# Routed rows kept as two planes of 16-bit halves and turned by a transposing DMA instead of TensorE

## What is computed

```
scores = softmax(xt @ gate_w.T)                    # 8 experts
top_vals, idx = top_k(scores, 2)
xs = xt[:, None, :] * weights[:, :, None]          # each token goes out twice, scaled
for e in range(8):
    h  = silu(xs @ w1[e].T + b1[e])
    x2 = h @ w2[e].T + b2[e]
    x3 = xs @ w3[e].T + b3[e]
    y += sum(x2 * x3 * (idx == e))
z = silu(xt @ sw1.T) * (xt @ sw2.T) @ sw3.T        # the shared expert
x = x + gb * (y + z)
```

## Time and profile before

| | us |
|---|---|
| median of 3 runs (2061.04 to 2063.82) | 2062.91 |
| the profiled execution, its own time | 2061.47 |
| its span, first to last instruction | 2059.7 |
| scatter stage, about | 1700 to 1842 |
| expert stage, first matmul of a tile to last accumulating DMA | 1844 to 2056 |

### The profile page before, as it was taken

How to read it: one execution, slowest core, us unless ns; L and a number is a source line. 1 busy time by engine, 2 the same in 40 slices (tenths; PEclk the granted TensorE clock), 3 DMA queues, 4 the chain that set the end, 5 groups by cost and what they waited for, 6 DMA issues and landing times.

```text
span 2059.7 us, 25386 instructions
## 1 busy us (share of the span) xinstructions
PE 1815.1 (88%) x6768; PEld 829.6 (40%) x6768; DVE 1923.7 (93%) x1820; ACT 1598.3 (78%) x3362; POOL 1796.3 (87%) x612
## 2 busy tenths in 40 slices
PE   7888898989797979888888989898976899999997
PEld 3323332424242423232323333332422356569996
DVE  7999999999999999999999999999999988857775
ACT  5886779898989898877788898989896744546664
POOL 5689999999999999999999999999999943545555
PEclk9998898989898989898998989898987899999999
DMA  7745454444545353536263535454445334635555
GB/s 268 229 139 145 110 137 111 129 115 112 133 110 127 106 129 106 140 88 164 68 160 89 143 92 136 111 135 115 116 105 149 100 129 137 253 134 88 97 94 75
DMA packets 140653, 263.93 MB, mean 128 GB/s; under 512 B 21840, under 2 KB 44368, under 8 KB 139488
## 3 DMA queue, kind: packets, MB, share of 16 engines
q1 hardware_dynamic: 125920, 240.58, 43.7%
q0 software_dynamic: 13296, 17.80, 5.1%
q10 hardware_dynamic: 1296, 3.93, 0.5%
HBM read 193.10 MB, written 70.19 MB: 128 GB/s over the span
## 4 chain that ended last, share of the span: by engine, by line
PE 26%; ACT 22%; DVE 19%; issue 17%; POOL 12%; DMA 4%; SPq 1%; DVEq 0%; ACTq 0%; POOLq 0%; PEldq 0%
DVE hst L1935 13%; ACT psum L1399 8%; POOL hst L1058 8%; DVE dbu L1914 5%; PE psum L2739 4%; PE psum L2495 4%; ACT dbu L1431 3%; PE psum L2925 3%; PE psum L2934 2%; PE psum L2753 2%; PE psum L2945 2%; POOL dbu L1046 2%; DMA out_x<-h,target_u 2%; PE psum L2415 1%; ACT sp_tmp L1368 1%
## 5 line engine op out<-in xcount | busy, mean ns | idle before, releaser
L1058 POOL TENSOR_TENSOR hst<-hst,c_rep 128x2048 f32<-128x2048 f32 x254 | 1145.4, 4535 | 3.9 <-ACT state L1385 3.6
L1399 ACT ACTIVATE psum<-dt_rep,neg_a 128x512 f32<-128x512 f32 (+1 forms) x1024 | 659.9, 676 | 122.7 <-DVE hst L1935 118.2
L1935 DVE TENSOR_TENSOR_SCAN hst<-psum,state,dbu 128x1024 f32<-128x1024 f32 x264 | 604.3, 2328 | 0.5 <-DVE score L2012 0.4
L1935 DVE TENSOR_TENSOR_SCAN hst<-psum,dbu 128x1024 f32<-128x1024 f32 x248 | 554.5, 2270 | 10.7 <-ACT psum L1399 10.6
L1914 DVE TENSOR_TENSOR dbu<-psum,b_rep 128x2048 f32<-128x2048 f32 x177 | 400.5, 2263 | 5.2 <-PE psum L2480 5.2
L1046 POOL TENSOR_TENSOR dbu<-dtu_rep,b_rep 128x2048 f32<-128x2048 f32 x79 | 359.4, 4549 | 8.6 <-DMA dtu_rep<-dtu_scratch 5.3
L2495 PE MATMUL psum<-hst,same 128*32 128x512 f32 x2048 | 268.8, 672 | 42.9 <-POOL hst L1058 42.9
L2480 PE MATMUL psum<-dt,same 32*128 32x512 f32 x354 | 216.5, 693 | 101.8 <-DVE dbu L1914 92.4
L2427 PE MATMUL psum<-xp,taps 128*128 128x512 f32 x512 | 237.6, 607 | 7.2 <-ACT sp_tmp L1365 6.6
L1189 POOL DMA_INDIRECT out_x<-h,target_u x71 | 111.5, 1570 | 107.1 <-issue 60.2
L1431 ACT ACTIVATE dbu<-first_decay,dbu,state 128x1 f32<-128x1 f32 x504 | 160.0, 376 | 20.8 <-DVE dbu L1914 19.4
(11 more groups left out here) (246 smaller groups left out, 2619.8 us busy)
## 6 DMA issues: line engine op xcount, KB each, us to landing
dt_rep<-dt_scratch SPq DMA_DIRECT2D x256, 256.0 KB, 4.8
dtu_rep<-dtu_scratch SPq DMA_DIRECT2D x316, 64.0 KB, 1.9
taps<-taps_scratch SPq DMA_DIRECT2D x64, 256.0 KB, 5.1
b_rep<-bc_scratch SPq DMA_DIRECT2D x64, 256.0 KB, 4.8
c_rep<-bc_scratch SPq DMA_DIRECT2D x64, 256.0 KB, 7.7
dt_scratch<-dt SPq DMA_DIRECT2D x48, 256.0 KB, 6.1
h<-slot_scratch SPq DMA_DIRECT2D x71, 129.5 KB, 2.6
sp_tmp<-t_scratch SPq DMA_DIRECT2D x16, 512.0 KB, 6.8
```

The lines of the kernel that those rows point to most:

```text
L1058: nc.gpsimd.tensor_tensor(h, h, c_rep[q % 2][:], ALU.mult).then_inc(prod_done, 1)
L1399: nc.scalar.activation(psum[:, PS_A + i, kept], dt_rep[:, G % 2, j, kept], ACT.Exp, scale=neg_a[:, q % 2, u, i:i + 1]).then_inc(exp_done, 1)
L1935: nc.vector.tensor_tensor_scan(both(hst[:, U % RING, groups, :]), both(psum[:, PS_A + 2 * pair:PS_A + 2 * pair + 2, :]), both(dbu[:, U % D ...
```

## The change

The rows in DRAM get 272 words instead of 259: the first 256 words hold the 256 float32 values as two planes of 16-bit halves, all first halves and then all second halves, and behind them stand the token number and flags. ScalarE first scales into a new buffer `weighed`, and then one more activation per `scale_tokens` splits 512 rows into the two planes of `send`. SyncE loads a tile with two DMAs: a transposing one of 128 rows by 512 halves into `turned_halves`, and a small one of 128 rows by 3 words into `xt_meta`. ScalarE's `join_halves` puts the two halves of each value side by side, SBUF to SBUF, in `xtT`, which has four buffers now. `turn_tile` and `copy_tile` are gone.

```
-ROW = DM + 1 + BATCH
+META = 1 + BATCH
+ROW = DM + 16
...
-                sp.dma_start(xt[:, s % 4, :], slot_dram[bass.ds(rows[s], P)]).then_inc(xt_loaded[s % 4], 16)
+                nc.sync.dma_start_transpose(turned_halves[:, s % 4].rearrange("p b (k c) -> p (b k) c", k=KD),
+                                            slot_halves[bass.ds(rows[s], P), 0:2 * DM]).then_inc(xt_loaded[s % 4], 16)
+                sp.dma_start(xt_meta[:, s % 4, :], slot_dram[bass.ds(rows[s], P), DM:DM + META]
+                             ).then_inc(xt_loaded[s % 4], 16)
...
             for s in range(TILES - 4):
                 sp.wait_ge(target_kept, s + 1)
                 sp.wait_ge(gate_done, s + 1)
+                sp.wait_ge(xtT_copied, s + 1)
...
+                if m >= 1:
+                    act.wait_ge(scaled, (NT + 3) * m)
...
-                    nc.scalar.activation(send[:, m % 4, tt, 0:DM], normed(p, tt), ACT.Copy, scale=weight[:, k, t:t + 1]
+                    nc.scalar.activation(weighed[:, tt, :], normed(p, tt), ACT.Copy, scale=weight[:, k, t:t + 1]
...
+                act.wait_ge(scaled, (NT + 3) * m + NT + 2)
+                nc.scalar.activation(send_halves[:, m % 4], weighed_halves, ACT.Copy).then_inc(scaled, 1)
...
-            def copy_tile(s):
-                act.wait_ge(xt_turned, s + 1)
-                if s >= 2:
-                    act.wait_ge(hx_full, s - 1)
-                nc.scalar.activation(xtT[:, s % 2, :], psum[:, s % 2, 0:DM], ACT.Copy).then_inc(xtT_copied, 1)
+            def join_halves(s):
+                act.wait_ge(xt_loaded[s % 4], 32 * (s // 4 + 1))
+                if s >= 4:
+                    act.wait_ge(hx_full, s - 3)
+                nc.scalar.activation(xtT_halves[:, s % 4], turned_halves[:, s % 4].rearrange("p b d -> p d b"), ACT.Copy
+                                     ).then_inc(xtT_copied, 1)
...
                 silu_tile(s)
-                if s + 1 < TILES:
-                    copy_tile(s + 1)
+                if s + 2 < TILES:
+                    join_halves(s + 2)
...
-            def turn_tile(s):
-                pe.wait_ge(xt_loaded[s % 4], 16 * (s // 4 + 1))
-                if s >= 2:
-                    pe.wait_ge(xtT_copied, s - 1)
-                for k in range(KD):
-                    ins = nc.tensor.transpose(psum[:, s % 2, k * P:(k + 1) * P], xt[:, s % 4, k * P:(k + 1) * P], ident[:])
-                ins.then_inc(xt_turned, 1)
...
             for s in range(TILES):
                 hidden_gate(s)
                 hidden_linear(s)
-                if s + 1 < TILES:
-                    turn_tile(s + 1)
                 if s > 0:
                     result(s - 1)
```

More of the change, by code:

```diff
@@ L10 @@
 U32 = mybir.dt.uint32
+U16 = mybir.dt.uint16
 I32 = mybir.dt.int32
@@ L215, in mixer_and_experts @@
         slot_dram = dram("slot_scratch", (SPARE + NE * P, ROW))
+        slot_halves = slot_dram.bitcast(U16)
+        slot_words = slot_dram.bitcast(U32)
         trash_dram = dram("trash_scratch", (NE * P, ROW))
@@ L391, in mixer_and_experts @@
         yt = part(8, 4, 1)
-        xtT = part(12, 2, 1)
+        xtT = part(12, 4, 1)
+        xtT_halves = xtT.bitcast(U16).rearrange("p n (d b) -> p n d b", b=2)
         hsT = part(16, 2, 1)
-        xt = flat[:, 18 * DM:18 * DM + 4 * ROW].rearrange("p (n d) -> p n d", n=4)
+        turned_halves = part(18, 4, 1).bitcast(U16).rearrange("p n (b d) -> p n b d", b=2)
+        xt_meta = flat[:, 22 * DM:22 * DM + 4 * META].rearrange("p (n d) -> p n d", n=4)
         row_gate = part(24, 2, 1)
@@ L398, in mixer_and_experts @@
         w1 = sb3("w1", [P, 2, KD, DM])
+        weighed = sb3("weighed", [P, NT, DM])
+        weighed_halves = weighed[:].bitcast(U16).rearrange("p t (d b) -> p t d b", b=2)
+        send_words = send[:].bitcast(U32)
+        send_halves = send[:].bitcast(U16)[:, :, :, 0:2 * DM].rearrange("p m t (b d) -> p m t d b", b=2)
         ffn.close()
@@ L1152, in scatter @@
                 pool.wait_ge(a_slots, m + 1)
-                pool.wait_ge(scaled, (NT + 2) * (m + 1))
+                pool.wait_ge(scaled, (NT + 3) * (m + 1))
                 for tt in range(NT):
                     nc.gpsimd.indirect_dma_start(
-                        slot_dram, bass.IndirectOffsetOnAxis(ap=slot_u[:, k, n * NT + tt:n * NT + tt + 1], axis=0),
-                        send[:, m % 4, tt, :], None).then_inc(y_stored[tt] if m == 0 else scattered[m % 4], 16)
+                        slot_words, bass.IndirectOffsetOnAxis(ap=slot_u[:, k, n * NT + tt:n * NT + tt + 1], axis=0),
+                        send_words[:, m % 4, tt, :], None).then_inc(y_stored[tt] if m == 0 else scattered[m % 4], 16)
             constants()
@@ L1736, in scale_tokens @@
                     t = n * NT + tt
-                    nc.scalar.activation(send[:, m % 4, tt, 0:DM], normed(p, tt), ACT.Copy, scale=weight[:, k, t:t + 1]
+                    nc.scalar.activation(weighed[:, tt, :], normed(p, tt), ACT.Copy, scale=weight[:, k, t:t + 1]
                                          ).then_inc(scaled, 1)
                 nc.scalar.activation(send[:, m % 4, :, DM], token_no[:, rows_of(n)], ACT.Copy).then_inc(scaled, 1)
-                nc.scalar.activation(send[:, m % 4, :, DM + 1:ROW],
+                nc.scalar.activation(send[:, m % 4, :, DM + 1:DM + META],
                                      batch_flag[:, n // SEG:n // SEG + 1, :].broadcast_to((P, NT, BATCH)), ACT.Copy
                                      ).then_inc(scaled, 1)
+                act.wait_ge(scaled, (NT + 3) * m + NT + 2)
+                nc.scalar.activation(send_halves[:, m % 4], weighed_halves, ACT.Copy).then_inc(scaled, 1)
             turned(2)
@@ L1830, in begin_gate @@
             def begin_gate(s):
-                act.wait_ge(xt_loaded[s % 4], 16 * (s // 4 + 1))
+                act.wait_ge(xt_loaded[s % 4], 32 * (s // 4 + 1))
                 if s >= 2:
                     act.wait_ge(gated, s - 1)
-                nc.scalar.activation(row_gate[:, s % 2, :], fmod[:, 0, 3, :], ACT.Copy, scale=xt[:, s % 4, DM + 1:DM + 2]
+                nc.scalar.activation(row_gate[:, s % 2, :], fmod[:, 0, 3, :], ACT.Copy, scale=xt_meta[:, s % 4, 1:2]
                                      ).then_inc(gate_begun, 1)
@@ L1842, in _ @@
                 rows_landed(act, m)
-            copy_tile(0)
+            join_halves(0)
+            join_halves(1)
             begin_gate(0)
@@ L2325, in bias_hidden @@
                                         b3[:, bass.ds(expert_of[s], 1), :], ALU.add).then_inc(hx_done, 1)
-                nc.vector.tensor_copy(target_u[:, s % IDS:s % IDS + 1], xt[:, s % 4, DM:DM + 1]).then_inc(target_kept, 1)
+                nc.vector.tensor_copy(target_u[:, s % IDS:s % IDS + 1], xt_meta[:, s % 4, 0:1]).then_inc(target_kept, 1)
             def gate_rows(s):
                 dve.wait_ge(gate_begun, s + 1)
-                nc.vector.scalar_tensor_tensor(row_gate[:, s % 2, :], fmod[:, 1, 3, :], xt[:, s % 4, DM + 2:DM + 3],
+                nc.vector.scalar_tensor_tensor(row_gate[:, s % 2, :], fmod[:, 1, 3, :], xt_meta[:, s % 4, 2:3],
                                                row_gate[:, s % 2, :], ALU.mult, ALU.add).then_inc(gate_done, 1)
@@ L2925, in hidden_gate @@
                         ins = nc.tensor.matmul(psum[:, 4 + s % 2, m * P:(m + 1) * P], w1[:, s % 2, k, m * P:(m + 1) * P],
-                                               xtT[:, s % 2, k * P:(k + 1) * P],
+                                               xtT[:, s % 4, k * P:(k + 1) * P],
                                                start=(m == 0 and k == 0), stop=(m == KD - 1 and k == KD - 1))
@@ L2933, in hidden_linear @@
                 for k in range(KD):
-                    ins = nc.tensor.matmul(psum[:, 2 + s % 2, 0:DM], xtT[:, s % 2, k * P:(k + 1) * P],
+                    ins = nc.tensor.matmul(psum[:, 2 + s % 2, 0:DM], xtT[:, s % 4, k * P:(k + 1) * P],
                                            w13[:, bass.ds(expert_of[s] * KD + k, 1), DM:2 * DM
```

2 lines of the change are left out of this document (removed).

## The result

The changed kernel takes 2186.85 us (median of 4 runs, 2185.31 to 2190.12), the kernel before 2062.49 (4 runs, 2061.04 to 2063.82) on the same chip: a ratio of 1.0606 [1.0594, 1.0619]. I had forecast 2071.5 and a range of 2058 to 2110. The direction was right, the size wrong by 115 us.

A forecast was written before the change was run, and what follows sets the result against it. It took TensorE (202 us) and GpSimd's landing waits (some 195) as nearly equal bounds of the expert stage. 2061.47 + 4.5 + 0.5 - 4.1 + 7.8 = 2070.2, plus 1.44 to the median: 2071.5 forecast, range 2058 to 2110.

The forecast's parts named there:

- the scatter stage: Stage before the expert stage: 16 added splits on ScalarE at 1.9 us each, making the start 4.5 us later.
- my 2.1 to 6.8 us: Scatter stage: bounds on the later start, 2.1 if all the splits' lateness is absorbed, 6.8 if none is.
- Its second half, how much lies on the path: Scatter stage: of some 34 us of splits most lies beside TensorE; 4.5 us lands on the path.
- The first tile: From last scatter landing to first matmul: transpose and copy go, second issue, slower load and join come; + 0.5 us.
- GpSimd takes over: Expert stage: with TensorE at 2.62 us a tile GpSimd's waits set the pace; 4.1 of 15.6 us gained.
- The loads and the landings: Expert stage: a tile's two loads take 0.9 us of the DMA engines, landings come 0.2 us later; + 7.8 us.
- my own prices: Expert stage: each us of longer landing costs GpSimd half on 62 steps and all of it on 8.
- + 3.7 forecast: Expert stage: the terms for GpSimd's pace, - 4.1 us, and later landings, + 7.8 us, taken together.
- my upper bound: Expert stage's transposing load: 512 pieces of 256 bytes, each at a whole packet's 57 ns, 1.8 us a tile.
- the loads become the bound: Rival, expert stage: the load pair brings the DMA engines to 3.4 us a tile; 2082 to 2130 us, chance 0.2.
- Two small sums: Scatter stage: 8.4 us added less 3.45 idle, put at 4.7 us; transposing load: 27% lost, 0.5 us put at 0.65.

The follow-up runs named there:

- the kernel with plain loads: The changed kernel with the transposing load replaced by a plain one of the same bytes: 2179.13 us, ratio 1.0495; with the split walked plane by plane too, 2075.56, 0.9996.
- turning put back: Two transposes a tile of a constant, result unread, put back on TensorE in the plane-order kernel: 2076.35 us, ratio 0.9996.
- looser waits: The plane-order kernel with GpSimd waiting for tile s - 3's landing, for s - 1 and s - 2 too where the expert changes: 2058.28 us; same on the control, 2073.88.
- the plane-order kernel: The changed kernel with plain loads for the transposing ones and the split walking plane by plane, writing runs of 256 halves: 2075.56 us, ratio 0.9996.
- the control: The kernel before with one edit: GpSimd's wait for the previous tile's landing takes the larger of the loaded count and 16; 2076.96 us, ratio 1.0003.
- the kernels that the split bounds: The changed kernel, 2186.85 us, and the changed kernel with its transposing load replaced by a plain one, split order kept, 2179.13 us.

## Why the prediction was wrong

**The step that failed** is the price of the split in "the scatter stage": "The zero fill of 4144 values takes 3.66 us, 0.83 ns each beyond some 0.2 us, so one is 1.9 us". It is 9.28. The fill writes a run; the split as it was written jumps 512 bytes with each half. The row that I took was right for the element count and said nothing on the order, and I looked for no bound on it: my 2.1 to 6.8 us were bounds on how much is absorbed. Walked plane by plane the same activation takes 1.91 us, the forecast's value. The Trainium skill has the rule ("Advanced Engine Details and Errata", section "SBUF Cachelines"): SBUF has lines of 16 bytes, and an access pattern that goes to another line each time pays a penalty. The measured step agrees with it, between jumps of 8 bytes at 0.63 us and 32 bytes at 2.48 us for 512 halves. Two things differ: the section speaks of accesses, and here reading by turns adds 0.23 us where writing adds 7.32; and it wants two hits on a line, which every fourth half has, at 1.33 us for 512 of them against 0.63 in a run.

**Its second half, how much lies on the path,** was too high at 1.9 us (4.5 forecast, 0.6 to 1.6 seen, less than can be told) and meant nothing at 9.28: from one weighing to the next are 11.30 us (1930.05 to 1941.35), 16 times that is 181 us, ScalarE becomes the stage's bound, and 88% of the extra is paid. I had written that ScalarE is idle about half of this stage; 16 x 7.4 = 118 us more in a stage of that length uses up the idle half and leaves nothing to hide behind.

**The first tile,** + 0.5: from the last scatter to the first matmul it is 7.58 us against 7.16, + 0.4. Right.

**GpSimd takes over.** Right in kind, and shown twice in the kernel with plain loads: turning put back costs nothing, and with looser waits 15.6 us come back, give or take the 3.5. Between changes the steps are 2.49 us with plain loads (1963.37 to 1975.83 in the plane-order kernel is five of them), as forecast. The size, - 4.1, stays open: from first to last accumulating DMA the three kernels with plain loads and the old waits have 200.8, 197.8 and 201.9 us, the control 201.8. One execution each, and they scatter by as much as the term.

**The loads and the landings.** The pair takes 0.85 us of the DMA engines (0.9 forecast), but a landing is 0.4 us later, not 0.2, which is outside what I had allowed. By my own prices 0.4 us would be 62 x 0.2 + 8 x 0.4 = 15.6 us and the stage + 11.5. It is + 4.3 from the first matmul to the last accumulating DMA (215.3 against 211.0), with + 3.7 forecast. So the sum came out nearly right by luck, from two terms that weren't both right. In the measure of the forecast itself, from the first to the last accumulating DMA, the stage went from 199.05 to 206.17 us, + 7.1 and not + 3.7; what hides it is that the first of them now comes 9.2 us behind the first matmul and not 12.0. Of the 7.1 us, 4.5 lie in the eight steps at a change, which have grown from 4.96 to 5.52 us in the mean.

What the transposing form costs over a plain load was only compared across two chips: from first to last accumulating DMA 206.2 against 200.8 us, 5.4 us. No run sets the two beside each other on one chip, so that the transposing load is what delays the landings is not shown. Its place in the DMA engines is surer. With plain loads, from 1975 to 2170 us, the queues have

```profile
q0 software_dynamic: 9792, 8.92, 39.3%
q1 hardware_dynamic: 18432, 8.50, 20.1%
```

which is 0.61 us a tile against 0.85, and 288 packets a tile against 688. The pieces of 256 bytes that my upper bound supposed would be 512 packets and fit that count; the price of 57 ns each doesn't, for a packet of the hardware queue takes 27.7% of 200 us x 16 / 44688 = 20 ns. The sentence of the Trainium skill that such DMAs are as fast as plain ones ("Advanced Engine Details and Errata", section "X-Bar Transpose (TRN2)") doesn't hold for tiles of this size here. Issuing one takes 1.20 us on SyncE, a plain one 0.33.

**The range** missed for one reason: no case let ScalarE become the bound of the scatter stage. Its upper end came from the rival "the loads become the bound", which stopped at 2130 and looked in the wrong place.

**Two small sums** are off, and nothing hung on them: 8.4 less 3.45 us is 4.95, not 4.7, and a load that loses 27% of its time goes from 0.5 to 0.69 us, not 0.65.

**Left open:** the changed kernel itself with the plane order, without and with the looser waits; both fixes were only shown with plain loads, on tiles that aren't turned. With both, an estimate from the parts is a gain of 15.6 us over the kernel before less the 5.4 us of the transposing load, some 10 us.

## What to carry to other kernels

When an added instruction has no like in the trace, match its walk as well as its size: an output pattern whose innermost step leaves the 16 bytes just written made 2048 halves cost 9.3 us instead of 1.9, and swapping two loops of the pattern mended it. Bound such a price before asking what hides it; 16 x 7.4 us had nowhere to hide. And where two engines' paths have nearly one length, shorten both or neither: 15.6 us of TensorE were worth nothing alone, looser waits on GpSimd nothing alone, and both together all of it, in the kernel with plain loads.

## What the runs showed of the hardware

- Writing halves by turns to places 32 to 512 bytes apart adds 3.6 ns to each on ScalarE; 32 and 512 bytes cost the same, 8 bytes nothing. At 512 bytes it adds 0.9 ns to each float32 on ScalarE, 3.6 ns to each half on GpSimd ((9.20 - 1.90) / 2048), and 1.7 on VectorE ((4.68 - 1.23) / 2048).
- On ScalarE each coming to another 16 bytes takes 4.4 ns for halves, however few are written there: 256 times in 1.33 us, 512 in 2.48, 2048 in 9.23. The 16 bytes are worked out from these three, not measured by jumps of 16.
- Reading by turns from two planes 512 bytes apart adds 0.1 ns a half on ScalarE ((2.14 - 1.91) / 2048).
- Where TensorE idled half of the time beside the splits, its granted clock was 0.81 to 0.83; in the expert stage, with 47.70 of 50 us busy, it was 1.00.
- What separates two chips can vanish: the kernel before has its last scatter at 1836.72 us on one and 1851.15 (the control) on another, and the kernels that the split bounds have 1957.51 and 1956.92. Each is one execution. A difference of 14 us between chips vanishes here when ScalarE sets the pace; I didn't follow where it comes from.
